# Early router products, held-back expert weights, result rows summed by VectorE, scores ahead of the output projection

## The reference, cut to what matters

```
# blocks 0, 2 and 3: attention with 12 heads of width 16 ("narrow"), in block 3 beside a "quantum" attention
attn = softmax(q @ k.T * scale) @ v          # block 0 also RMS-normalises q and k per head

# block 0, ffn: grouped attention with 12 heads of width 64 ("wide"), then a mixture of 16 experts, two per token
logits = x2d @ w_router                      # (1088, 16)
probs = softmax(logits); vals, idx = top_k(probs, 2); vals = vals / sum(vals)
for e in range(16):
    gate, up = split(x2d @ w_gate_up[e])
    out = out + combine[:, e:e+1] * ((silu(gate) * up) @ w_down[e])

# block 3, ffn: four experts, one per token
top = argmax(x @ Wg + bg)                    # (1088, 4)
out = (gelu(x @ W1[top] + b1[top])) @ W2[top] + b2[top]
```

## Time and profile before

| | |
|---|---|
| time, median of 3 runs | 966.59 us (963.37 to 973.13) |
| profiled execution | 969.99 us, span 968.2 us |
| mean granted clock of TensorE | 0.96 of full |
| PE busy | 877.8 us, 91%, 6254 matmul instructions |
| DVE, ACT, POOL busy | 445.9 us, 387.8 us, 186.3 us |
| row writes of f3 | four of 384 KB land in 3.4 us, one of 96 KB in 3.5 us |
| expert weights of moe | 16 loads of 576 KB and 16 of 288 KB |

### The profile page before, as it was taken

The page is one execution under the profiler, slowest core; times in us unless marked ns, Lnnn a source line. Parts: engine busy times, 40 slices in busy tenths (PEclk is TensorE's granted clock), DMA queues, the critical chain, the costliest instruction groups (busy, mean ns, idle before and its releaser), DMA issues. The chain is left out here.

```text
span 968.2 us, 17121 instructions
## 1 busy us (share of the span) xinstructions
PE 877.8 (91%) x6254; PEld 625.9 (65%) x6255; DVE 445.9 (46%) x896; ACT 387.8 (40%) x857; POOL 186.3 (19%) x207
## 2 busy tenths in 40 slices
PE   6899878999998799999899789998999999988997
PEld 5566656677765467777677466764686566656776
DVE  5456676777735212222168665551104566623011
ACT  2356553454431023233253764544152455522332
POOL 0600002544500134444200012220000000001232
PEclk9989999999997699999999898999999999996999
DMA  8000000000008961112330029000000211102111
GB/s 283 1 1 1 1 2 1 1 2 1 1 2 231 259 175 49 49 45 48 95 96 1 1 69 226 2 1 27 1 1 1 57 49 50 50 14 85 48 52 34
DMA packets 30641, 51.10 MB, mean 53 GB/s; under 512 B 3750, under 2 KB 23752, under 8 KB 30572
## 3 DMA queue, kind: packets, MB, share of 16 engines
q1 hardware_dynamic: 22140, 36.09, 13.2%
q0 software_dynamic: 4416, 9.84, 3.7%
q10 hardware_dynamic: 4016, 4.23, 1.3%
HBM read 43.30 MB, written 6.83 MB: 52 GB/s over the span
## 5 line engine op out<-in xcount | busy, mean ns | idle before, releaser
L78 PE MATMUL banks<-con 128*128 128x512 f32 (+1 forms) x212 | 103.3, 603 | 3.8 <-PEq L84 1.7
L1817 PE MATMUL banks<-moe_wu,moe_xf 96*128 x256 | 91.2, 501 | 1.5 <-issue 1.0
L622 PE MATMUL banks<-x,a_wqkv 96*96 96x272 f32 x288 | 76.6, 405 | 1.9 <-PEq L84 1.9
L1817 PEld LDWEIGHTS banks<-moe_wu,moe_xf 96*128 96x128 f32 x256 | 47.1, 194 | 31.3 <-issue 4.3
L78 PEld LDWEIGHTS banks<-con 128*128 128x128 f32 x212 | 41.4, 209 | 31.8 <-issue 27.9
L921 ACT ACTIVATE a_vt<-banks 102x384 f32<-102x384 f32 x96 | 42.3, 488 | 43.9 <-PE banks L698 43.1
L622 PEld LDWEIGHTS banks<-x,a_wqkv 96*96 96x96 f32 x288 | 46.8, 169 | 20.1 <-issue 5.7
L142 ACT ACTIVATE ln_sq<-x 96x544 f32<-96x544 f32 x32 | 21.0, 656 | 95.6 <-DVE x L134 95.5
L2118 DVE TENSOR_TENSOR moe_hid<-banks,moe_gs 128x384 f32<-128x384 f32 x32 | 17.8, 557 | 79.6 <-PE banks L1817 79.6
L698 PE MATMUL banks<-con,a_vx 96*102 96x96 f32 x384 | 45.4, 263 | 7.7 <-ACT a_vt L921 5.5
L1979 POOL DMA_INDIRECT moe_xs<-moe_x_rows,moe_taken x32 | 31.1, 972 | 87.6 <-PE banks L1801 56.6
(11 more groups left out here) (404 smaller groups left out, 1789.3 us busy)
## 6 DMA issues: line engine op xcount, KB each, us to landing
moe_wu<-in_moe_up SPq DMA_DIRECT2D x16, 576.0 KB, 12.7
f_w<-in_f_e SPq DMA_DIRECT2D x10, 576.0 KB, 14.0
moe_wd<-in_moe_down SPq DMA_DIRECT2D x16, 288.0 KB, 14.4
patch_px<-in_patches SPq DMA_DIRECT2D x4, 768.0 KB, 9.7
f_wu<-in_f_up SPq DMA_DIRECT2D x4, 582.0 KB
f_wd<-in_f_down SPq DMA_DIRECT2D x4, 576.0 KB
f_x_rows<-f_xtok ACTq DMA_DIRECT2D x4, 384.0 KB, 3.4
a_wqkv<-in_a_wqkv SPq DMA_DIRECT2D x3, 432.0 KB, 8.7
```

Source lines behind the costliest of these rows:

```text
L78: self.nc.tensor.matmul(self.ps[bank][:, 0:width], self.ident, self.con[:, 0:width], start=True, stop=True)
L622: last = nc.tensor.matmul(ps[2 + m][0:HD, 0:CW], wqkv[:, a, j * D + m * HD:j * D + (m + 1) * HD], chunk(x, c)[:, a], start=a == 0, stop=a ...
L1817: last = nc.tensor.matmul(ps[2 + 2 * p + u][:, 0:BW], xf[0:KU[a], p, a], wu[0:KU[a], bass.ds(e, 1), a, u * BW:(u + 1) * BW].rearrange("p e ...
```

## The change

It has six parts. (1) a0 gets one idle product between the first scores and the first value turn. (2) In all three narrow attentions the scores of the next chunk's first group are issued ahead of `project_out`, and DVE's shift of that group ahead of the two adds. (3) The logits of the first six of nine router tiles are made in the stage before the routed one: in g0 in place of the two idle products (L1415), in a3 three tiles before and three behind the last norm variance, where they also add an idle product's narrower form; the logits stay in the upper half of a PSUM bank over the barrier. (4) In the routed head three tiles of logits are left; DVE copies the early ones first, and PE waits for that copy before its transposes; the idle products are laid out anew (5, 3 become 3, 6 in moe; 2, 0 become 1, 2 in f3). (5) SP loads 7 experts instead of 12 ahead of the gathers, and the other nine one by one, each awaited before the next is issued. (6) DVE sums the two copies of the result rows in SBUF for a pair of tiles, PE then only transposes them, and two narrow idle products are added between.

```diff
+EARLY = 6
+    def route_early(self, pe, router, src, bank, lo, hi):
+        E = router.wr.shape[2]
+        for t in range(lo, hi):
+            for a in range(2):
+                last = self.nc.tensor.matmul(self.ps[bank][:, 256 + t * E:256 + (t + 1) * E], src[:, a, t * 128:(t + 1) * 128], router.wr[:, a],
+                                             start=a == 0, stop=a == 1)
+        return last
 # narrow attention, PE
+            scores(0)
+            if rms:
+                env.idle_products(1, 1)
             for c in range(NC):
-                scores(2 * c)
                 turn_values(2 * c)
...
                     project_v(c + 1, 1)
+                    scores(2 * c + 2)
                 else:
                     env.idle_products(1, 2)
                 project_out(c)
             if not left:
                 env.idle_products(1, 2)
                 ln.mean(pe, L)
-                env.idle_products(1, 2)
+                if router is None:
+                    env.idle_products(1, 2)
+                else:
+                    pe.wait_ge(router.small_in, 48)
+                    pe.wait_ge(ln.ready, L)
+                    env.route_early(pe, router, x, 3, 0, EARLY // 2)
+                    env.idle_products(1, 2, 256)
                 ln.var(pe, L)
+            if router is not None:
+                env.route_early(pe, router, x, 3, EARLY // 2, EARLY)
             env.idle_products(2, 2)
 # narrow attention, DVE
-                shift(2 * c)
+                if c == 0:
+                    shift(0)
...
                     spread_values(c + 1)
+                    shift(2 * c + 2)
                 for m in range(2):
                     dve.wait_ge(o_proj, 2 * c + m + 1)
 # wide attention, PE, last chunk
-                    env.idle_products(2, 0)
+                    pe.wait_ge(router.small_in, 16)
+                    pe.wait_ge(n2.ready, 2 * c)
+                    env.route_early(pe, router, x2, 0, 0, EARLY)
 # routed experts, SP
-            FIRST = 12
+            FIRST = 7
...
-                experts.load(sp, range(FIRST, E))
             for e in range(FIRST, E):
+                experts.load(sp, range(e, e + 1))
                 sp.wait_ge(w_in[e], 32)
                 sp.sem_inc(w_ready, 1)
 # routed experts, PE
-            for t in range(NR):
+            for t in range(EARLY, NR):
...
             last.then_inc(routed, 1)
+            pe.wait_ge(early_read, 1)
...
-            env.idle_products(5 if top2 else 2, 0)
+            env.idle_products(3 if top2 else 1, 0)
             pe.wait_ge(prefix_ready, 1)
...
-            env.idle_products(3 if top2 else 0, 0)
+            env.idle_products(6 if top2 else 2, 0)
...
             def turn_out(t):
-                pe.wait_ge(y_back[t // 2], 32)
+                pe.wait_ge(summed, t // 2 + 1)
...
-                    for k in range(K):
-                        last = nc.tensor.matmul(ps[2 + t % 4][0:HD, a * RT:a * RT + n], yb[k][0:n, t, a * HD:(a + 1) * HD], env.ident[0:n, 0:n],
-                                                start=k == 0, stop=k == K - 1)
+                    last = nc.tensor.transpose(ps[2 + t % 4][0:HD, a * RT:a * RT + n], yb[0][0:n, t, a * HD:(a + 1) * HD], env.ident[0:n, 0:n])
...
                 for t in range(5):
                     turn_out(t)
+                    if t % 2:
+                        env.idle_products(1, 7, width=256)
 # routed experts, DVE
-            dve.wait_ge(routed, 1)
-            for lo, hi, n in ((0, NR - 1, RT), (NR - 1, NR, LAST)):
-                logits = ps[7][0:n, lo * E:hi * E].rearrange("p (t e) -> p t e", e=E)
+            early = ps[0 if top2 else 3][:, 256:512]
+            for lo, hi, n, bank in ((0, EARLY, RT, early), (EARLY, NR - 1, RT, ps[7]), (NR - 1, NR, LAST, ps[7])):
+                if lo == EARLY:
+                    dve.wait_ge(routed, 1)
+                logits = bank[0:n, lo * E:hi * E].rearrange("p (t e) -> p t e", e=E)
...
+            def sum_rows(b):
+                dve.wait_ge(y_back[b], 32)
+                n, w = rows(2 * b), min(2, NR - 2 * b)
+                both = [yb[k][0:n, 2 * b:2 * b + w] for k in range(2)]
+                V.tensor_tensor(both[0], both[0], both[1], ALU.add).then_inc(summed, 1)
...
-                for t in range(5):
-                    add(t)
+                sum_rows(0)
+                sum_rows(1)
+                add(0)
+                add(1)
+                sum_rows(2)
+                add(2)
+                add(3)
+                sum_rows(3)
+                add(4)
                 ln.centre(dve, 0)
+                sum_rows(4)
```

More of the change, by code:

```diff
@@ L540, in stage_tokens, with stage_narrow_attention @@
         return ln
-def stage_narrow_attention(env, name, weights, rms=False, quantum=False, response=None, ahead=(), before=None, left=0, first_rms=None):
+def stage_narrow_attention(env, name, weights, rms=False, quantum=False, response=None, ahead=(), before=None, left=0, first_rms=None, router=None):
     nc = env.nc
@@ L1243, in scale, with stage_wide_attention @@
                                            self.rs[:, c % 2], ALU.mult, ALU.mult).then_inc(self.ready, 1)
-def stage_wide_attention(env, name, weights, n1, before, ahead=()):
+def stage_wide_attention(env, name, weights, n1, before, router, ahead=()):
     nc = env.nc
@@ L1693, in stage_routed_ffn @@
         xt_ready, xt_moved, rows_out = sem("xt_ready"), sem("xt_moved"), sem("rows_out")
+        early_read = sem("early_read")
         lists_ready, taken_ready, listed_read = sem("lists_ready"), sem("taken_ready"), sem("listed_read")
@@ L1700, in stage_routed_ffn @@
         numbered, row_taken = sem("numbered"), sem("row_taken")
-        out_turned, added, ones_ready = sem("out_turned"), sem("added"), sem("ones_ready")
+        out_turned, added, ones_ready, summed = sem("out_turned"), sem("added"), sem("ones_ready"), sem("summed")
         ln = Norm(env, name + "_ln", env.x, added, [-(-(c + 1) * CW // RT) for c in range(NC)], var_banks=(1, 6, 7, 1), left=2 if norm_out else 0)
@@ L2017, in _ @@
                     last = V.tensor_tensor(lg[0:n, lo:hi], logits, bg[0:n, None, :].broadcast_to([n, hi - lo, E]), ALU.add)
+                if lo == 0:
+                    last.then_inc(early_read, 1)
             link(last)
@@ L2861, in build @@
             env.end_stage()
-            stage_wide_attention(env, "g0", g0, n1, last)
+            stage_wide_attention(env, "g0", g0, n1, last, moe_router)
             env.end_stage()
@@ L2884, in build @@
                 f3 = ExpertWeights(env, inner, "f3", of("f3"))
-                stage_narrow_attention(env, "a3", a3, quantum=True, ahead=[f3_router, f3])
+                stage_narrow_attention(env, "a3", a3, quantum=True, ahead=[f3_router, f3], router=f3_router)
                 env.end_stage()
```

## The result

The changed kernel takes **952.66 us** (951.07 to 953.71, 4 runs) against 966.2 (963.37 to 973.13, 4 runs) on the same chip: ratio 0.9854 [0.9806, 0.9902]. Forecast: 951 (942 to 963).

| stage | before | after | difference | forecast |
|---|---|---|---|---|
| start | 40.40 | 39.88 | −0.5 | 0 |
| a0 | 112.30 | 107.81 | −4.5 | −2.8 |
| g0 | 141.25 | 146.24 | +5.0 | +2.8 |
| moe | 201.95 | 188.48 | −13.5 | −13.6 |
| next two | 77.30 | 76.73 | −0.6 | 0 |

A forecast was written before the change was run, and what follows sets the result against it. It took PE's list as nearly closed (busy 91%), with the routed heads as serial chains where PE waits or does nothing useful. Terms summed to −15.2 on the profiled 969.99 us, giving 954.8, less 3.4: 951 us, range 942 to 963.

The forecast's parts named there:

- a0 product: In a0, a product of constants in PE's wait keeps the clock up for the second scores: −2.8 us.
- Scores and shift first: At chunk ends of the narrow attentions, the reordering stays hidden behind PE's list: 0, bounds −1.5 and +1.5 us.
- Early logits in g0: In g0, 24 logit instructions replace two idle products, costing their length and a possible clock fall: +2.8 us, bounds +1.2 and +4.6.
- Logits out of moe's head: In moe's head, 24 of 36 logit instructions leave: 3.84 us saved.
- lists at full clock: In moe's head, a longer idle block keeps the clock up for the lists: −3.2 us, bounds −3.9 and +4.
- Gather: In moe's head, fewer expert weights in the DMA queue let the first gather land sooner: −4.0 us, bounds −5.0 and −2.
- Serial loads: In moe's loop, nine later experts loaded one by one, about 6.6 us each, arrive in time: 0.
- slower rival: In moe, the later experts come too late, with a stall of 35 us: 986 us, chance 0.05.
- Tail: In moe's tail, DVE sums the rows and PE only transposes: −2.0 us, bounds −3.5 and +2.
- a3 and f3: Logits moved from f3's head into a3's end: +2.2 before the barrier, −3.8 behind it, −1.6 us overall.
- narrow products cool the engine everywhere: Clock falls: g0 +4.6, moe −8.4 with lists at half clock, tail +1, f3 +1.5; 962 us, chance 0.20.
- the head is set by something beside the chain: Row writes, waiting on POOL, set the head; only a0 and the tail gain, against g0's cost: 965 us, chance 0.05.

The follow-up runs named there:

- e1: The kernel before with one edit, the product of constants in the first chunk of a0: 966.33 us, ratio 0.9964.
- e3: The changed kernel without early logits in g0, its two idle products back and all nine tiles' logits in moe's head: 952.19 us.
- after_again: The changed kernel unaltered, run again beside the others of its chip: 955.62 us, ratio 0.9866.
- e4: The changed kernel with twelve experts loaded ahead of the gathers, as before, instead of seven: 958.72 us, ratio 0.9905.
- e8: The changed kernel with the second block of products of constants in moe's head at six instructions instead of twelve: 950.57 us.
- e10: The changed kernel with four experts loaded ahead of the first gather instead of seven, so twelve serial loads: 949.09 us.
- e11: The changed kernel with the five row writes of f3's head issued by SyncE instead of ScalarE: 949.56 us, ratio 0.9805.
- e5: The changed kernel with g0's early logits moved from mid-chunk to the stage's end, replacing products of constants there: 949.10 us.
- e7: The changed kernel with moe's tail as before, PE turning and summing the result rows: 957.39 us, ratio 0.9843.
- e9: The changed kernel with each row write of f3's head issued by ScalarE right behind its move: 957.03 us, ratio 0.9852.
- e2: The changed kernel with projection and adds ahead of scores and shift again in all three narrow attentions: 956.26 us.
- best2: The changed kernel with g0's logits at its end, four experts ahead, f3's row writes on SyncE, 16 constants before moe's lists: 941.93 us.

## Why the prediction was right, and where its steps were not

The total came out within 2 us, and moe by 0.1. The direction and the three main reasons (product in a0, held-back weights, sums on DVE) are borne out; the closeness is luck. moe's −13.5 compares one trace with one, and other traces of the same two moe codes would give −10.9 to −19.0. Between the two traces the spans fell by 19.5, not 15.2, and the profiled execution took 951.07 where the sum gave 954.8 for it; the medians fell by 13.5. Inside, several steps were off and partly hid each other.

- **a0 product**, −2.8: −2.85 alone (e1). Right, and for its reason. The other 1.6 us of a0 in the table are one stretch of half clock near 100 us which the profiled run lacks, and 0.3 of reordering.
- **Scores and shift first**, 0 ± 1.5: −1.4 over three stages, of which 0.8 in a3. Near the bound. I had excluded a gain because the exponent waits for the value turn; which wait gave way was not followed up.
- **Early logits in g0**, +2.8: +5.0, outside the bound of 4.6, and a named sign of being wrong. The plain length was right (2.85 for an estimate of 3.07), and PE was held for 2.70 us (270.80 to 273.50) instead of 1.82, 0.9 more; the clock was priced at 1.5 and cost about 4.1 (5.0 − 0.9), since it stayed at half for 10.2 us and not for half of a0's 6.8. The row that I had leant on for the risk, busy PE at 0.50, was the right one: the window from 274.60 has PE busy 9.44 of 10.10 us at 0.50. By the rule of the Trainium skill (TensorE: Matmul & The Clock Gate, Part 1: The HAM clock gate), under which sustained work keeps the full rate, the part would have cost 1.25. This trace does not bear that out: PE was busy for all 3.60 us up to 274.40, and the clock fell at 274.5.
- **Logits out of moe's head**, −3.84, and **lists at full clock**, −3.2: each made its own stretch shorter by that much (e3: gather 3.6 us later; lists 7.90 to 4.55), and neither moved the end of moe by more than its spread (e3 188.69; after_again with lists of 7.00 us 188.17, against 188.48). The full clock in the lists is no firm result either: they took 6.9 to 7.3 us in after_again, e4, e8, e10 and e11, and 6.3 in e5. The failed step is the addition: I took every piece of the serial head as a piece of its end. The rows are turned at 28.9 to 30.5 us in all kernels with seven experts ahead, for gathers issued anywhere from 22.5 to 27.6.
- **Gather**, −4.0, from 8.3 to 5.5 us: −2.8 as a duration. As a part it is far more: with twelve ahead again, and everything else kept, first down comes 7.5 us later (e4). It had been counted as one term of four, and is the one on which the head hangs: its estimate followed the row of the weights, but its share in the end of moe was set too low.
- **Serial loads**, 0: right (no wait; 5.1 to 7.0 us each, mean 5.8; estimate 6.6). The slower rival falls, also with twelve loads. The estimate of 5.3 us from the fixed cost in the Trainium skill (DMA: Bandwidth & Descriptors, Anatomy of one DMA) is 0.5 below the mean of this trace; that section describes DMAs issued by GpSimd, and these loads are issued by SyncE.
- **Tail**, −2.0: −1.6 by the two traces at full clock, −2.8 by e7 against e9, where 3.4 us of the tail are at half clock. Right.
- **a3 and f3**, −1.6: −5.0. Before the barrier +0.5 instead of +2.2. 0.8 of the difference is the reordering in a3, which the sum had at 0; without it (e2) the stage took 1.3 more than before, so part of the 24 logit instructions seems to have filled waits, which no run tests by itself. Behind it, −5.6 instead of −3.8. The limit was named rightly (the gather now waits for row writes), but its size was taken from the logits alone, while the last write was issued 4.2 us earlier (13.0 behind the barrier against 17.2), since the ranks, behind which its transposes stand, came 6.0 earlier and not 4.7. Gather 4.5 earlier (17.3 against 21.8), first rows turned 5.8 earlier (20.5 against 26.3). And −5.6 goes with the place of the clock's falls in this trace; six other traces with the same f3 have 92.7 to 92.9, −7.9.

Of the rivals, "the gather gains nothing" was wrong, "narrow products cool the engine everywhere" was right for g0 in every trace with the logits in its middle, and the lists at half clock that it expected stand in six of the twelve traces behind the change, but its time was wrong: moe lost 10.9 or more, not 8.4. The rival with the smallest chance beside the slow loads, "the head is set by something beside the chain", had the mechanism in part: the queue of weights and the third block of constants set the turned rows, not the chain up to the gather. It had the price wrong, since holding back the weights moved just that limit. What stays open: which of the waits the reordering removes, why the DMA was through with the same weights sooner in some traces than in others, and where in a run the clock falls, which decides up to 4.0 us in f3 (91.2, 92.8 or 95.2) and 8.6 in a0 (107.8 to 116.4) with the same code.

## What to carry to other kernels

A serial head that ends in a DMA isn't the sum of its pieces: find when the DMA could have answered at the earliest, and count nothing for pieces that end before. Hold back what fills the queue first; only behind that can the compute steps of the head be worth something (no run here shows by how much), and work moved out of it must be free where it goes. Products of constants are work too: at half clock a block placed as a cover becomes the last wait.

## What the runs showed of the hardware that was not expected

- 24 products with 16 columns in 2.85 us, in an otherwise dense stretch, were followed by 10.2 us at 0.50 (13.7 in e2) in every profiled run that had them in the middle of g0. In those that had none there (before, e1, e3, e5, best2) the stage keeps full clock up to its last 1.0 us. The stage takes 145.9 to 146.3 us with them there (147.6 in e2) and 140.8 to 141.3 without.
- The same kernel's lists took 4.55 us in one execution and 7.00 in another, and the same a0 107.8 in five traces, 109.1 in two, 112.4 in one and 116.2 to 116.4 in three.
- An issued DMA on ScalarE between two moves set the next move back by 0.44 us, four times (e9).
- The first rows of moe were turned 8.3 to 9.0 us behind the issue of their gather with twelve experts' weights in the queue (before, e1, e4), 3.9 to 6.6 with seven, and 2.9 where the weights were through before the issue (e3).
